# The head layer norm's reciprocal root split in two: Abs_reciprocal_sqrt on ScalarE replaced by Sqrt on ScalarE and a reciprocal on VectorE

## The reference

```python
def _ln(x, g, b, eps=1e-05):
    mu = jnp.mean(x, axis=-1, keepdims=True)
    var = jnp.mean(jnp.square(x - mu), axis=-1, keepdims=True)
    return (x - mu) * jax.lax.rsqrt(var + eps) * g + b
...
q = _ln(silu(x @ Wq).reshape(B, L, H, D), q_g, q_b)
kv = silu(x @ Wkv)
k = _ln(kv[..., :C].reshape(B, L, H, D), k_g, k_b).reshape(B, L, C)
```

## Time and profile before

| what | value |
|---|---|
| median of 3 runs | 1127.54 us (1126.61 to 1127.72) |
| profiled execution, its own time | 1127.54 us |
| its span, first to last instruction | 1125.7 us |
| TensorE busy | 952.7 us |
| VectorE busy | 797.3 us |
| GpSimd busy | 725.3 us |
| ScalarE busy | 486.4 us |
| granted TensorE clock, mean | 0.952 |

### The profile page before, as it was taken

How to read it: one execution, slowest core, us unless ns; L and a number is a source line. 1 busy time by engine, 2 the same in 40 slices (tenths; PEclk the granted TensorE clock), 3 DMA queues, 4 the chain that set the end, 5 groups by cost and what they waited for, 6 DMA issues and landing times.

```text
span 1125.7 us, 25018 instructions
## 1 busy us (share of the span) xinstructions
PE 952.7 (85%) x8131; PEld 768.9 (68%) x8132; DVE 797.3 (71%) x1147; ACT 486.4 (43%) x1149; POOL 725.3 (64%) x469
## 2 busy tenths in 40 slices
PE   9993199989989989787877579999999999999960
PEld 5552198978978978665656467777777777777740
DVE  5889999999999998558888854454445445444435
ACT  3697434445545554345665413233223223322325
POOL 4687999999999999401000346666666666667532
PEclk9997599999999999899999689999999999999985
DMA  3271212221221221487765512222222222222227
GB/s 107 70 138 27 65 29 66 70 70 47 70 65 51 70 62 55 185 301 252 232 215 169 174 39 40 47 42 44 45 46 43 42 47 42 45 44 42 33 30 298
DMA packets 69916, 100.24 MB, mean 89 GB/s; under 512 B 9248, under 2 KB 51680, under 8 KB 68928
## 3 DMA queue, kind: packets, MB, share of 16 engines
q1 hardware_dynamic: 53968, 81.04, 22.7%
q0 software_dynamic: 15904, 18.66, 10.6%
HBM read 73.82 MB, written 26.25 MB: 89 GB/s over the span
## 4 chain that ended last, share of the span: by engine, by line
PE 44%; POOL 19%; issue 17%; DVE 10%; ACT 5%; DMA 3%; POOLq 0%; SPq 0%; DVEq 0%; ACTq 0%
PE psum L797 18%; PE psum L805 11%; POOL mid L1270 10%; PE psum L807 5%; POOL arena L1275 2%; DVE arena L1634 2%; PE psum L600 2%; POOL arena L1261 2%; PE psum L684 2%; POOL arena L1281 2%; PE psum L789 1%; ACT arena L1181 1%; PE psum L733 1%; POOL arena L1224 1%; DMA sum_dram<-arena,mid 1%
## 5 line engine op out<-in xcount | busy, mean ns | idle before, releaser
L797 PEld LDWEIGHTS psum<-arena 128*128 x3408 | 239.0, 98 | 75.2 <-issue 8.8
L797 PE MATMUL psum<-arena 128*128 128x128 f16 x3408 | 286.7, 220 | 4.1 <-DVE arena L1790 1.6
L620 PE MATMUL psum<-consts,mid 128*128 128x128 f32 x2108 | 245.1, 277 | 43.9 <-POOL mid L1270 43.9
L620 PEld LDWEIGHTS psum<-consts,mid 128*128 128x128 f32 x2108 | 240.1, 193 | 53.7 <-issue 40.2
L1270 POOL TENSOR_TENSOR mid<-arena 128x2304 f32<-128x2304 f32 (+1 forms) x62 | 251.3, 4075 | 9.4 <-POOL arena L1261 7.6
L805 PE MATMUL psum<-arena 128*128 x568 | 215.0, 380 | 4.9 <-DVE arena L1781 1.2
L1349 POOL DMA_INDIRECT sum_dram<-arena,mid x71 | 141.8, 1997 | 43.6 <-issue 19.5
L1790 DVE SCALAR_TENSOR_TENSOR arena<-psum,arena 128x256 f32<-128x256 f32 x71 | 34.3, 484 | 186.1 <-ACT arena L1153 110.9
L1153 ACT ACTIVATE arena<-psum,arena 128x256 f32<-128x256 f32 x71 | 33.6, 473 | 296.4 <-PE psum L807 296.4
L1473 DVE TENSOR_REDUCE arena<-mid 128x272 f32<-128x4624 f32 x32 | 158.9, 4965 | 1.7 <-ACT mid L954 1.4
L807 PE MATMUL psum<-arena 128*128 x568 | 154.8, 273 | 0.0
(11 more groups left out here) (198 smaller groups left out, 1477.7 us busy)
## 6 DMA issues: line engine op xcount, KB each, us to landing
arena<-w_t SPq DMA_DIRECT2D x64, 256.0 KB, 2.8
arena<-w_t SPq DMA_DIRECT2D x16, 1024.0 KB, 10.3
arena<-x SPq DMA_DIRECT2D x32, 128.0 KB, 2.1
arena<-x_dram SPq DMA_DIRECT2D x8, 512.0 KB, 5.2
arena<-ctx_t SPq DMA_DIRECT2D x8, 512.0 KB, 6.0
arena<-ctx SPq DMA_DIRECT2D x8, 512.0 KB, 6.7
x_dram<-mid SPq DMA_DIRECT2D x8, 512.0 KB, 3.3
arena<-sum_dram SPq DMA_DIRECT2D x8, 512.0 KB, 7.5
```

The lines of the kernel that those rows point to most:

```text
L620: last = nc.tensor.matmul(psum[:, u, c * P:(c + 1) * P], av_prod[half][:, w, c * P:(c + 1) * P], ident, start=(a + w == 0 and c == 0), sto ...
L797: last = nc.tensor.matmul(dst, block_of(w, e, 0, c * F + j * P, P), x[:, u, c * P:(c + 1) * P], start=(k == 0 and c == 0), stop=(k == 2 an ...
```

## The change

ScalarE's function in `head_roots` becomes Sqrt, and its result goes into a new PSUM tile `head_root[j]`, in the bank of `head_var[j]` from column 256 on, instead of into `head_r` in SBUF. VectorE then makes `head_r` as the reciprocal of that tile, at the front of `newton_begin`, and waits for its own result before the first Newton product. Since ScalarE no longer writes `head_r`, its two waits for the previous group's products (`rstd_heads`, `k_scaled`) go. The counts of `newton_step` go from three to four per group.

```diff
+        head_root = [psum[:, 6 - j % 2, 256:256 + GROUP * 2 * H].rearrange("p (n x) -> p n x", x=2 * H) for j in range(GROUPS)]
...
             def head_roots(j):
                 act.wait_ge(var_eps, j + 1)
-                if j:
-                    act.wait_ge(rstd_heads, j)
-                    act.wait_ge(k_scaled, j)
-                nc.scalar.activation(head_r, head_var[j], ACT.Abs_reciprocal_sqrt).then_inc(root_done, 1)
+                nc.scalar.activation(head_root[j], head_var[j], ACT.Sqrt).then_inc(root_done, 1)
...
                 dve.wait_ge(root_done, j + 1)
+                done(nc.vector.reciprocal(head_r, head_root[j]), newton_step, 4 * j + 1)
                 nc.vector.tensor_tensor(var, var, head_r, ALU.mult).then_inc(newton_step, 1)
 
             def newton_end(j):
 
                 var = head_var[j]
-                dve.wait_ge(newton_step, 3 * j + 1)
-                done(nc.vector.tensor_tensor(var, var, head_r, ALU.mult), newton_step, 3 * j + 2)
+                dve.wait_ge(newton_step, 4 * j + 2)
+                done(nc.vector.tensor_tensor(var, var, head_r, ALU.mult), newton_step, 4 * j + 3)
...
-                dve.wait_ge(newton_step, 3 * j + 3)
+                dve.wait_ge(newton_step, 4 * j + 4)
```

## The result

| | changed kernel | kernel before, same chip | ratio, 95% interval |
|---|---|---|---|
| first measurement | 1133.93 us (1132.31 to 1134.26) | 1127.07 us (1126.39 to 1127.72) | 1.0052 (1.0035 to 1.0069) |
| second measurement (`after_again`) | 1132.07 us | 1129.35 us | 1.0022 (1.0003 to 1.0041) |

The change makes the kernel slower, by some 2.5 to 6 us (0.22% and 0.52%). The forecast was 1132.8 us with a range of 1129.2 to 1134.9. The profiled execution took 1129.99 us, with a span of 1128.1 us; it is quicker than the runs around it, which matters further down.

The account below looks back on a forecast made before the run. No engine bounds the projection throughout; GpSimd's fixed-time window stage passes on any delay of its start. 4 x 1.99 = 7.96 us, less 2.67 of slacks, is 5.3; 1127.5 + 5.3 = 1132.8 us, range 1129.2 to 1134.9.

Parts of the forecast that it names:

- What one reciprocal costs: VectorE, each group: 1.92 us for 256 elements plus 0.02 and 0.05, R = 1.99 us; 1.6 to 2.3 held likely.
- the sum: Delay at 116 us: 4 x 1.99 = 7.96 us of VectorE time, less 2.67 of slacks, is 5.3 us.
- The sum's lower end: Outer bound of the sum: with 0.5 us per reciprocal, only +0.3 us, from a rest of group 1 and group 3.
- The four slacks: Squares of steps 16 and 19, step 29's gains, step 0's peak: take 1.05, 0.20, 1.06, 0.36 us, together 2.67.
- The window stage passes it on: GpSimd, 116 to 457 us: fixed time from its first L1281, no slack, so the 5.3 us reach the end.
- the sign: End of the window stage: VectorE's wait before the last L1503 would still be over 4 us.
- B: Explanation set up after the first measurement: stages behind the window add their own delay, before + 6 to 7 us.
- The projection did not swallow its three: Rival, 30 to 102 us: idle time absorbs groups 0 to 2, only group 3's 1.63 us stays, 1129.2 us; chance 0.12.
- The loads stayed four: Forecast: four 1283 ns table loads at L878. Rival: Sqrt shares Silu's set, three roots' loads go, 1129.0 us; chance 0.06.
- The cheap reciprocal: Rival, VectorE: reciprocal costs as a plain instruction, +0.3 us, 1127.8 us; chance 0.03.
- The clock did not fall at project(23): Rival, TensorE in the projection: a wait of about 2.2 us drops its clock, costing 1.9 us, 1134.7 us; chance 0.08.

Follow-up runs that it names:

- recip_twice: Changed kernel with every group's reciprocal made twice; 1139.55 against 1128.22 us for the kernel before, ratio 1.0099 (1.0076 to 1.0122).
- last_group_only: Kernel before, with Sqrt and reciprocal in group 3 only, groups 0 to 2 as before; ratio 1.0009 (0.9989 to 1.0029).
- recip_no_newton: Changed kernel without the three Newton instructions, the two products replaced by copies; ratio to the kernel before 1.0010 (0.9993 to 1.0026).
- first_groups_only: Kernel before, with Sqrt and reciprocal in groups 0 to 2 only, group 3 as before; ratio 1.0040 (1.0019 to 1.0061).
- recip_direct: Changed kernel without Newton steps or copies, reciprocal in two halves straight into query and key tiles, `key_rstd` moved to SBUF; ratio to the kernel before 1.0100.
- ars_no_newton: Kernel before (Abs_reciprocal_sqrt) without the three Newton instructions, the two products replaced by copies; ratio 1.0019 (1.0006 to 1.0032).
- ars_plus_recip: Kernel before plus an unused reciprocal on VectorE before the first Newton product; 1132.63 against 1129.35 us, ratio 1.0030 (1.0014 to 1.0047).

## Why the prediction came out as it did

**What one reciprocal costs: mis-sized.** The prediction took R = 1.99 us, from the slope of the longer pair of instructions, 7.0 ns per element. Measured are 1.78: the slope from 32 to 256 elements is (1748 - 355) / 224 = 6.2 ns, between the two slopes that the earlier trace rows give. That is 0.21 too much in each group, 0.84 in the sum, and it is nearly all by which the sum was off. The two small additions, 0.02 for a PSUM operand and 0.05 for the wait, are 0.03 together as measured (1.78 from start to start, 1.748 for the instruction), and no run shows the first by itself. The sum's lower end has a slip: with 0.5 us for each reciprocal, the prediction's own slacks leave 0.30 + 0.14 = 0.44 and not 0.3.

The prediction set beside this an estimate of 2.13 us from the Trainium skill (VectorE: DVE Perf Modes, Walkthrough: the 8-slice pipeline in each mode), read as 8 cycles for an element. The 8 cycles were the prediction's reading of a repeat count. The trace doesn't agree with it: 1748 ns for 256 elements is less than that estimate.

**The four slacks: right.** They were read from the kernel before, and each was found in its place. The sum with the measured R is 4 x 1.78 - 2.67 = 4.45; the mark shows 4.43. Step by step:

| place | by the prediction's slacks, R = 1.78 | measured |
|---|---|---|
| square of step 16 | 1.78 - 1.05 = 0.73 | 0.71 |
| square of step 19 | 0.73 + 1.78 - 0.20 = 2.31 | 2.28 |
| first window product | 2.31 + 1.78 - 1.06 = 3.03 | 2.98 |
| first subtraction | 3.03 + 1.78 - 0.36 = 4.45 | 4.43 |

`recip_twice` tries the same sum at twice the cost, and it comes out to 0.05 us.

**The window stage passes it on: right, to about 1 us.** 4.43 at its start, 4.30 at its end, GpSimd's groups unchanged, and VectorE's wait at the end nearly as large (3.92 us, where the sign asked for over 4). The stage doesn't take a fixed time, though: between its two marks the shift grows by 1.13 us in `recip_twice` and by 0.82 in `last_group_only`, and shrinks by 0.50 in `recip_no_newton`. It is one wait of GpSimd's, for TensorE's first window sum. **GpSimd in the kernel before, then TensorE and GpSimd in `recip_twice`**, timelines:

```profile
141.78 8.10 POOL L1270 TENSOR_TENSOR mid<-arena 128x2304 f32<-128x2304 f32 x2 [1.46 <-PE psum L620]
```
```profile
147.82 10.75 PE L621 MATMUL psum<-consts,mid 128*128 128x128 f32 x68 [44.53 <-POOL mid L1268]
```
```profile
155.15 8.11 POOL L1268 TENSOR_TENSOR mid<-arena 128x2304 f32<-128x2304 f32 x2 [2.47 <-PE psum L621]
```

The first window sum takes 9.74 us before, 10.75 here, 10.44 in `last_group_only` and 9.29 in `recip_no_newton`, at a mean granted clock of 0.79 before and 0.72 here, after a stretch at 0.50 in both. GpSimd's wait changes by the same 1.0, 0.7 and -0.5 us.

**The end: inside the range.** With 4.4 the forecast would have been 1127.54 + 4.4 = 1131.9. The first measurement gave 1133.93 and the second 1132.07, each beside another median of the kernel before. Both intervals hold 4.4 us. B isn't needed for either, and nothing in the traces shows a later stage that adds to the delay in every run; that some of the first measurement's 5.9 is more than scatter stays possible. Against that speak the executions on record: 37 of the changed kernel have a median of 1133.03 us, 81 of the kernel before, run beside the experiments, one of 1128.71, 4.3 less. They mix chips and times, so they give no interval. That the forecast of 1132.8 lies so near the first measurement is in part luck: R was 0.84 us too large in the sum, and that measurement lies above what the marks give.

**The rivals.** The projection did not swallow its three: 3.01 us of `first_groups_only` arrive at the mark. The loads stayed four. The cheap reciprocal fell with 1748 ns. The clock did not fall at project(23), though its wait was 1.96 us, near the 2.2 foreseen; `recip_twice` shows that such a fall can come in the projection, and that its price of some 1.3 us (3.29 against 1.98) did not reach the end, because TensorE wasn't the late one there. The rival's 1.9 us was thus both unsure to come and, in `recip_twice`, hidden.

**What stays open:** why the store's landing and the time behind 457 us vary by up to some 4 us between single executions of kernels that agree until then, why the first window sum's length differs by 1.5 us, and why the clock fell after one wait of some 2 us and not after two others.

## What to carry to other kernels

A busy share of 71% doesn't say that an engine has room. Follow a delay through the hand-overs (here the squares of steps 16 and 19, the gains of step 29, the peak of step 0) and subtract each slack once. In this kernel that was good to a tenth of a us, and the unknown duration of the new instruction was the main error. And before an operand of VectorE is moved from PSUM to SBUF beside a busy GpSimd, count what it will wait: in `recip_direct` the place of one small tile cost 8.4 us, about twice what the whole change did.

## What the runs showed of the hardware

- **VectorE waits for GpSimd by where its operands lie.** 128x128 from SBUF to SBUF took between 226 and 4323 ns, to PSUM 280 to 285; 128x512 with both operands in SBUF a mean of 1474 ns, with one in PSUM 677. That GpSimd is what they wait for is read from the times: the same 128x128 copy takes 226 ns where GpSimd is idle (`ars_no_newton`, 110.50) and 4323 beside its work. The hold lasted past the end of one GpSimd instruction into the next (90.76 to 95.08, over L1245 and two of L1203).
- The Trainium skill (SBUF — State Buffer, Who interferes with whom) states that a VectorE instruction with two SBUF inputs contends with a GpSimd instruction that reads SBUF. It also states that a copy in a mode that uses both ports contends with GpSimd, and that whichever issues first has the shared pair of ports for its whole instruction while the other is blocked. The traces agree on which instructions are held: copies from SBUF to SBUF and tensor_tensor instructions with two SBUF inputs are; copies to PSUM and tensor_tensor instructions with one input in PSUM aren't. By that section of the Trainium skill the block lasts for one whole instruction of the other engine; the 4.32 us copy outlasted L1245's 1.73 us, so here the wait was longer than that.
- **VectorE's reciprocal, fp32:** 1748 ns (median) for 128x256 and 950 and 894 (means of four) for 128x128, beside the 355 of 128x32. From PSUM to SBUF and from SBUF to PSUM it was not held up by GpSimd: the eight of the changed kernel and of `ars_plus_recip` lie between 1747 and 1761 ns.
- **An output in PSUM instead of SBUF** spares ScalarE 15 ns on 128x256 (368 against 383).
- **TensorE's clock** kept 1.00 after waits of 1.96 us (changed kernel, 72.73) and 2.05 us (`recip_twice`, 76.78). After one of 1.98 us (`recip_twice`, 64.73) its mean from 66 to 70 us was 0.67, between the levels of 1.2 and 2.4 GHz.
